# Expert pages of 64 rows, two to a block, ranked on the chip by expert

## The reference, cut to what matters

```python
probs = sigmoid(x @ router_w.T + expert_bias)          # (2048, 160)
top_w, top_idx = top_k(probs, 8)
top_w = top_w / (sum(top_w) + 1e-09) * 2.5
h1 = silu(einsum('th,eih->eti', x, w_gate))            # per expert 256 -> 128
routed = einsum('eti,ehi->th', h1 * combine.T, w_down) # per expert 128 -> 256
shared = silu(x @ w_gate_shared.T) @ w_down_shared.T
return x + routed + shared
```

## Time and profile before

| | |
|---|---|
| time, median of 3 runs | 1448.95 us (1445.54 to 1453.1) |
| span of the profiled execution | 1580.3 us |
| phase 1 and 2, in that execution | 1051 us |
| block loop with its fill and drain | 474 us |
| final sum and output | 55 us |
| HBM read and written | 161 MB and 100 MB |

### The profile page before, as it was taken

The page is one execution under the profiler, slowest core; times in us unless marked ns, Lnnn a source line. Parts: engine busy times, 40 slices in busy tenths (PEclk is TensorE's granted clock), DMA queues, the critical chain, the costliest instruction groups (busy, mean ns, idle before and its releaser), DMA issues. The chain is left out here.

```text
span 1580.3 us, 32555 instructions
## 1 busy us (share of the span) xinstructions
PE 1369.1 (87%) x10653; PEld 1008.8 (64%) x10653; DVE 996.6 (63%) x2910; ACT 618.7 (39%) x1909; POOL 615.5 (39%) x797
## 2 busy tenths in 40 slices
PE   7999999999987989999998998677787887878846
PEld 4666676666754666666666666466676776767645
DVE  3766666666653578867887787546665655544447
ACT  3544545444443566655665565221111111133100
POOL 1101111011101146555655555545556565555630
PEclk9999999999996899999999999889999999998978
DMA  8534244243400011111111111278878777776758
GB/s 257 191 98 142 92 142 138 95 141 100 134 1 28 14 53 53 51 63 63 50 54 64 63 36 40 70 235 266 248 232 245 233 236 250 239 218 204 227 195 351
DMA packets 153404, 221.57 MB, mean 140 GB/s; under 512 B 23789, under 2 KB 111116, under 8 KB 151320
## 3 DMA queue, kind: packets, MB, share of 16 engines
q1 hardware_dynamic: 53912, 97.83, 19.5%
q10 hardware_dynamic: 79456, 86.96, 17.6%
q0 software_dynamic: 19872, 34.71, 6.1%
HBM read 161.16 MB, written 99.61 MB: 165 GB/s over the span
## 5 line engine op out<-in xcount | busy, mean ns | idle before, releaser
L898 POOL DMA_INDIRECT y_d<-y,xg x286 | 278.6, 974 | 200.5 <-DVE y L895 126.7
L890 PE MATMUL bank<-pTC,ex 128*128 128x256 f32 x572 | 193.6, 423 | 73.2 <-ACT ex L884 41.0
L872 DVE COPY ex<-bank 128x256 f32<-128x256 f32 x286 | 120.4, 421 | 173.2 <-PE bank L868 101.9
L884 ACT ACTIVATE ex<-bank 128x128 f32<-128x128 f32 x286 | 77.6, 277 | 381.3 <-PE bank L880 222.0
L880 PEld LDWEIGHTS bank<-ex,pTC 128*128 128x128 f32 x1144 | 184.2, 207 | 51.2 <-issue 34.8
L880 PE MATMUL bank<-ex,pTC 128*128 128x128 f32 x1144 | 190.9, 293 | 17.4 <-issue 16.9
L890 PEld LDWEIGHTS bank<-pTC,ex 128*128 128x128 f32 x572 | 93.2, 205 | 91.0 <-ACT ex L884 48.9
L707 POOL DMA_INDIRECT xs_d<-xw,slot_id x128 | 131.0, 1023 | 34.6 <-issue 30.5
L895 DVE COPY y<-bank 128x256 f32<-128x256 f32 x286 | 120.5, 421 | 30.3 <-PE bank L890 18.1
L406 ACT ACTIVATE ex<-bank,nmC 128x256 f32<-128x256 f32 x256 | 119.5, 488 | 8.6 <-DVE nmC L400 8.1
L868 PE MATMUL bank<-ident,xg 128*128 128x128 f32 x572 | 116.0, 287 | 3.9 <-DMA xg<-xs_d 3.9
(11 more groups left out here) (308 smaller groups left out, 2919.5 us busy)
## 6 DMA issues: line engine op xcount, KB each, us to landing
pTC<-in_wexp SPq DMA_DIRECT2D x286, 256.0 KB
xs_d<-zeros ACTq DMA_DIRECT2D x16, 2448.0 KB, 9.7
xg<-xs_d ACTq DMA_DIRECT2D x143, 272.0 KB
cT<-in_ctx SPq DMA_DIRECT2D x32, 512.0 KB, 3.6
xg<-y_d SPq DMA_DIRECT2D x6, 1024.0 KB, 12.4
y_d<-y,xg POOLq DMA_INDIRECT x286
ex<-y_d SPq DMA_DIRECT2D x3, 1024.0 KB, 15.5
xf_d<-xw SPq DMA_DIRECT2D x16, 128.0 KB, 2.7
```

What stands on the lines that cost most here:

```text
L872: T.done("dve", dve.tensor_copy(xgT[z][:, :, :], bk[:, 0:2 * P].rearrange("p (c n) -> p c n", c=2)))
L884: U.done("act", act.activation(h[z][:, :], bk[:, 0:P], ACT.Silu))
L890: D.done("pe", pe.matmul(bk[:, 0:DIM], h[z][:, :], w[z][:, DIM:2 * DIM], start=True, stop=True))
L898: pool.indirect_dma_start(out=y_d, out_offset=bass.IndirectOffsetOnAxis(ap=who, axis=0), in_=y[:, n, :], in_offset=None, bounds_check=last ...
```

## The change

Pages have 64 rows (`PAGE`), and 416 of them cover the worst case; a block of the loop takes two pages, so there are 208 blocks instead of 286. A page may belong to any expert, so that a block has two.

- Rows carry no expert number any more. `stage_f` can give an expert one or two new pages in a tile (`gap`, `more`, `need`).
- `count_pages` computes per tile, on DVE, which expert owns each page, from the running sums.
- `order_pages` ranks the 416 pages by owner at the end of `phase2`: counts and comparisons on DVE, two groups of small matrix products on PE, and six operations on one partition, which write two tables into SBUF: for each place the expert and the page.
- The sorted list is cut into 16 slots of 26 pages. Block `d` of a turn of 8 blocks takes the next page of slots `2d` and `2d+1`; each slot has its own weight buffer of 256 KB. Where the next page has the same owner, 1000 is added to its number, so that the load is out of bounds and moves nothing. 16 buffers instead of 8 are made from `pT` and from weights of `phase2`.
- `load_weights` reads two numbers and issues two transfers on SP per block. `load_rows` does the same on ACT: two transfers of 64 rows, at page numbers out of the second table, 12 blocks ahead.
- `up` makes four products of 64 columns instead of two of 128, `down` two products with 64 stationary columns each, into the lower and the upper half of the PSUM rows.
- `common_up`, `common_down` and `common_out` have other due times, so that some of the shared expert's work falls beside the ordering.

```diff
+PAGE = 64
+SLOTS = 16
+TURNS = -(-((PAIRS + EXPERTS * (PAGE - 1)) // PAGE) // SLOTS)
+PAGES = SLOTS * TURNS
+BLOCKS = PAGES // 2
@@ stage_f
-            link(dve.tensor_tensor(need[:, :], after, room[:, :], ALU.is_gt))
+            dve.tensor_copy(ends[z][:, 0:1], ends[1 - z][:, EXPERTS:EXPERTS + 1])
+            link(dve.tensor_tensor(gap, after, room[:, :], ALU.subtract))
+            link(dve.tensor_scalar(more[:, :], gap, 0.0, None, ALU.is_gt))
+            link(dve.scalar_tensor_tensor(out=need[:, :], in0=gap, scalar=float(PAGE), in1=more[:, :], op0=ALU.is_gt, op1=ALU.add))
@@ count_pages
+            for n, c in enumerate(unsure):
+                last = dve.scalar_tensor_tensor(out=(late[:, :], spot[:, 0, :])[n % 2], in0=ends[j % 2][:, 1:], scalar=page[:, c:c + 1], ...
@@ order_pages
+            link(dve.tensor_reduce(keys[:, 0, :], counts[:, :, :], AX.X, ALU.add))
+            for c in range(CHUNKS):
+                last = pe.matmul(bank[7][:, c * P:(c + 1) * P], bc(keys[:, 0, c:c + 1], 1, P), ident[:, :], start=True, stop=True)
+            for c in range(CHUNKS):
+                last = dve.scalar_tensor_tensor(out=junk[c % 2], in0=row, scalar=keys[:, 1, c:c + 1], ...
+                        dve.tensor_scalar(onehot[k], numbers, ranks[:, k:k + 1], None, ALU.is_equal).then_inc(s_sort, 1)
+            for c in range(CHUNKS):
+                last = pe.matmul(bank[7][0:1, 0:PAGES], keys[:, 1, c:c + 1], onehot[c], start=(c == 0), stop=(c == CHUNKS - 1))
...
+            sp.wait_ge(s_table, 1)
+            for n in range(SLOTS // 2):
+                load_weights(nc, a, table, n, w, s_w)
@@ experts
+    _, which = nc.values_load_multi_w_load_instructions(table[0][0:1, 2 * n:2 * n + 2], engines=[mybir.EngineType.SP])
+    for half, e in enumerate(which):
+        sp.dma_start(w[2 * d + half], a["wexp"][bass.ds(e, 1)].rearrange("a p n -> (a p) n"), bounds_check="skip_entire_dma").then_inc(s_w[d], 16)
@@ load_rows
-            act.dma_start(xg[:, d % DOUBLES, :, :], doubles[steps[d]]).then_inc(s_g[d % DOUBLES], 16)
+            _, which = nc.values_load_multi_w_load_instructions(table[1][0:1, 2 * n:2 * n + 2], engines=[mybir.EngineType.Activation])
+            for half, q in enumerate(which):
+                act.dma_start(xg[half * PAGE:(half + 1) * PAGE, n % FETCHED, :], pages[bass.ds(q, 1)].rearrange("a p n -> (a p) n"), ...
@@ up
-            for c in range(2):
-                last = pe.matmul(bk[:, 0:P], w[z][:, c * P:(c + 1) * P], xgT[z][:, c, :], start=(c == 0), stop=(c == 1))
+            for half in range(2):
+                cols = slice(half * PAGE, (half + 1) * PAGE)
+                for c in range(2):
+                    last = pe.matmul(bk[:, cols], w[2 * z + half][:, c * P:(c + 1) * P], xgT[z][:, c, cols], start=(c == 0), stop=(c == 1))
@@ down
-            D.done("pe", pe.matmul(bk[:, 0:DIM], h[z][:, :], w[z][:, DIM:2 * DIM], start=True, stop=True))
+            for half in range(2):
+                rows = slice(half * PAGE, (half + 1) * PAGE)
+                last = pe.matmul(bk[rows, 0:DIM], h[z][:, rows], w[2 * z + half][:, DIM:2 * DIM], start=True, stop=True)
```

More of the change, by code:

```diff
@@ L122, in phase2_weights @@
     return (tern, wf, wqd, wod, wka, wkb, wva, wvb, bqd, bkd, bvd, bod, lns, lnb, wh, bh, bg, wqk, bqk, osw, osb, wout, bout,
-            wgs, wds, wr, be, tri, ones, base, pairs, half), loads
+            wgs, wds, wr, be, tri, ones, owner, page, pairs, half), loads
 class Turns:
@@ L225, in phase2 @@
         (tern, wf, wqd, wod, wka, wkb, wva, wvb, bqd, bkd, bvd, bod, lns, lnb, wh, bh, bg, wqk, bqk, osw, osb, wout, bout,
-         wgs, wds, wr, be, tri, ones, base, pairs, half) = resident
+         wgs, wds, wr, be, tri, ones, owner, page, pairs, half) = resident
         s_set, s_max = sem("s_set2"), sem("s_max")
@@ L264, in phase2 @@
         before = pair("before", [P, EXPERTS])
+        more = sb("more", [P, EXPERTS])
         need = sb("need", [P, EXPERTS])
         grown = sb("grown", [P, 2, EXPERTS])
-        ends = pair("ends", [P, EXPERTS])
-        room, lift, origin = sb("room", [P, EXPERTS]), sb("lift", [P, EXPERTS]), base
+        ends = pair("ends", [P, 1 + EXPERTS])
+        room, lift, origin = sb("room", [P, EXPERTS]), sb("lift", [P, EXPERTS]), sb("origin", [P, EXPERTS])
+        counts, expert, keys = sb("counts", [P, CHUNKS, TILES]), sb("expert", [P, CHUNKS]), sb("keys", [P, 2, CHUNKS])
         fresh = sb("fresh", [P, 2, EXPERTS])
@@ L271, in phase2 @@
         spot = sb("spot", [P, 2, EXPERTS])
-        whole = sb("whole", [P, TOPK], U32)
+        gap = spot[:, 1, :]
+        s_ids, s_pages, s_sort = sem("s_page_ids"), sem("s_pages"), sem("s_sort")
         s_common = [sem(f"s_common{z}") for z in range(3)]
@@ L710, in stage_f, with count_pages @@
                 grow(j)
-        def first_weights():
+        def count_pages(j):
+            yield 273.00
+            few, many = P * TOPK * j // PAGE, (P * TOPK * (j + 1) + EXPERTS * (PAGE - 1)) // PAGE
+            unsure = [c for c in range(CHUNKS) if P * (c + 1) > few and P * c < many]
+            for n, c in enumerate(unsure):
+                last = dve.scalar_tensor_tensor(out=(late[:, :], spot[:, 0, :])[n % 2], in0=ends[j % 2][:, 1:], scalar=page[:, c:c + 1],
+                                                in1=owner[:, :] if j < TILES - 1 else ones_e[:, :], op0=ALU.is_le, op1=ALU.mult, accum_out=counts[:, c, j:j + 1])
+                if n % 2 and c < unsure[-1]:
+                    link(last)
+            R.done(j, "dve", last, "counted")
+            R.wait(dve, "counted", j)
@@ L713, in first_weights @@
             yield 83.87
-            sp.wait_ge(s_rows[0], 16 * TOPK)
-            with nc.allow_non_contiguous_dma(reason="one word of each page"):
-                sp.dma_start(todo_row[0:1, 0:EARLY], page_words(xs_d)[0:1, 0:EARLY, :].rearrange("p q o -> p (q o)")).then_inc(s_todo, 16)
-            sp.wait_ge(s_todo, 16)
+            sp.wait_ge(s_table, 1)
+            E.wait(sp, "yo", TILES - 1)
             D.wait(sp, "pv", TILES - 1)
-            for r in range(EARLY):
-                load_weights(sp, a, todo_row, r, w[r], s_w[r])
+            for n in range(SLOTS // 2):
+                load_weights(nc, a, table, n, w, s_w)
@@ L929, in experts @@
             act.wait_ge(s_rows[z], 16 * TOPK * TILES // 2)
-        for d in range(AHEAD):
-            load_rows(d)
-        with nc.allow_non_contiguous_dma(reason="one word of each page"):
-            sp.dma_start(todo_row[0:1, EARLY:PAGES], page_words(xs_d)[0:1, EARLY:PAGES, :].rearrange("p q o -> p (q o)")).then_inc(s_todo, 16)
-        sp.wait_ge(s_todo, 32)
-        for b in range(PAGES + DOWN):
-            if EARLY <= b < PAGES:
+        for n in range(AHEAD):
+            load_rows(n)
+        for b in range(BLOCKS + DOWN):
+            if DEEP <= b < BLOCKS:
                 load(b)
-            if b % 2 == 0 and b // 2 + AHEAD < half:
-                load_rows(b // 2 + AHEAD)
+            if b + AHEAD < BLOCKS:
+                load_rows(b + AHEAD)
             if DOWN <= b:
                 down(b - DOWN)
-            if UP <= b < PAGES + UP:
+            if UP <= b < BLOCKS + UP:
                 up(b - UP)
-            if b < PAGES:
+            if b < BLOCKS:
                 turn(b)
@@ L953, in experts @@
         g = [v.rearrange("p (k n) -> p k n", k=TOPK) for v in g]
-        s_row = [sem(f"s_row{z}") for z in range(RING)]
+        s_row, used = s_w, TURNS * 32
         s_sum = [sem(f"s_sum{z}") for z in range(2)]
```

167 lines of the change are left out of this document (102 added, 65 removed).

## The result

| | before | after |
|---|---|---|
| time, median | 1448.91 us | 1834.89 us (1833.59 to 1835.9) |
| ratio after / before | | 1.2652, 95% interval 1.2625 to 1.2679 |

The changed kernel is 26.5% slower. I had forecast 1531 us (5.7% slower) in a range of 1450 to 1580, so the sign was right and the time lies 255 us above the range.

A forecast was written before the change was run, and what follows sets the result against it. The prediction took PE, at 1.10 us a block and the granted clock, to bound the loop before. Replacing its 343 us by 396 and adding 29 for routing, ordering and prologue gave 1449 - 343 + 396 + 29 = 1531 us, range 1450 to 1580.

The forecast's parts named there:

- The clock: Granted clock in the changed loop taken as 0.97, making 376 us at full clock into 388 us.
- `turn`, `up`, `down`: PE's work per block of the changed loop: 0.22 + 0.87 + 0.72 = 1.81 us at the full clock.
- rival 1: Weight loads in `up` are hidden, so `up` stays at 0.45 us and the total is 1445 us; chance 0.12.
- rival 3: Half-array products of `down` don't overlap: `down` 1.04 us, block 2.13 us, total 1600 us; chance 0.09.
- ACT: ACT's reads, row-transfer issues, waits and silu in the changed loop: about 1.45 us a block, below PE's 1.81.
- The loop before: Without the recording's stops, the old loop takes 343 us, bound by PE at 1.10 us a block and the granted clock.
- Routing: Added DVE operations per tile, some 2 us each, mostly hidden by PE's other work: 3 us in all, between 0 and 12.
- Ordering: Ranking pages after the last `spot`, then 16 first loads, delays the barrier to about 1058 us: 13 us, bounds 5 and 20.
- Prologue: 15 blocks' row transfers on ACT ahead of the loop's first silu take 18 us: loss 13 us, bounds 6 and 18.
- Transfers and the skip: Loop's weight loads fall from 207 to 120, 54 to 31 MB; transfers hidden under PE before and after, gain worth nothing.
- Rival 2: Transfers bound the loop before, which takes 435 us unrecorded; lighter traffic pays, total 1439 us or 1427; chance 0.13.
- rival 4: The skip does nothing: 329 pages load 256 KB each, the loop takes 423 us, total 1558 us; chance 0.02.

The follow-up runs named there:

- e14: Changed kernel with the rows of 5 blocks instead of 12 issued ahead of the loop: 1826.86 us.
- e15: Changed kernel without its skip, every page with pairs loading its weights: 1837.12 us.
- e4: Changed kernel with `up` as four products of 128 columns, silu taking its own 64, result unchanged: 1582.2 us in one recorded execution.
- e8: The kernel of e4 (changed kernel with full columns in `up`), timed without recording: 1556.72 us, ratio 1.0730 to the kernel before.
- e9: Changed kernel with full columns in `up`, rows of 5 blocks ahead, and second pages' row transfers on SP instead of ACT: 1580.33 us, ratio 1.0881.
- e16: Changed kernel with full columns in `up` and the rows of 5 blocks instead of 12 ahead of the loop: 1538.87 us, ratio 1.0590.
- e2: Changed kernel with `down` as one product on the whole array, second page's weights left out: 1578.2 us in one recorded execution.
- e7: Changed kernel with 32 more products of 512 columns on PE in the prologue, results unused: 1557.5 and 1804.3 us.
- e10: The kernel of e7 (32 more PE products in the changed kernel's prologue), four more executions: 1557.7, 1746.8, 1795.0 and 1602.4 us.
- e3: Changed kernel with `up` and `down` both as in the kernel before, second page's weights left out: 1575.9 us in one recorded execution.
- e12: The kernel before, unchanged, in one more recorded execution: span 1445.9 us, without stops.
- e6: The kernel before with every weight load behind the first eight out of bounds, moving nothing: 1448.48 us, ratio 0.9989.
- e11: The kernel before, scattering 32 rows instead of 128 in 78 of 286 blocks, whose pages hold no pair: 1443.78 us, ratio 0.9934.

## Why the prediction was wrong, step by step

- **The clock, the step that failed.** "With the stops gone and PE without gaps I take 0.97." It was 0.50. The mixture of both new forms, which comes at the low level out of the prologue, never regained the full one, in eight executions (the result, e14, e15). With full columns in `up` it did in all thirteen (e4, e8, e9, e16), with `down` on the whole array in the one of e2; e7 and e10 show that the level and not the work makes the time. What in the two forms together keeps it low, the runs don't show. Against the loop at the full clock (2.00 us a block, set by ACT) this is (3.365 - 2.004) x 207 = 282 us. My argument, PE without gaps, was read from products of the old forms; in the low loop PE was busy in 600 of 600 us. Nor did the prediction ask what PE's stop at the barrier would do to the clock. The Trainium skill (page "TensorE: Matmul & The Clock Gate", section "What's actually happening") puts it that recent busyness of PE releases the throttle. This case disagrees if busyness is what the profile counts: 100% at 0.50 in the changed kernel, 67% at 0.99 in e3.
- **`turn`, `up`, `down` in clock cycles: right.** 0.22 + 0.87 + 0.72 = 1.81 us forecast; 3.38 / 2 = 1.69 from the low level's block, 0.22 + 0.94 + 0.58 = 1.74 in e7. `up` is bound by its weight loads, so rival 1 falls. The Trainium skill (same page, section "LDWEIGHTS (loading the stationary operand)") makes a load's ns its columns divided by 1.2, an estimate of 107 ns for 128 columns. The 0.11 us a pair at the full clock agrees; at the low level a pair takes 0.22. `down` came out under my lower bound of 0.61, so rival 3 falls too, and the change of tile shape costs `down` less than I had read from the earlier trace rows; a part of it falls to `up`, whose first pair in e7 takes 0.16 us instead of 0.11.
- **ACT: too small.** 1.45 us a block forecast, 2.00 measured. I took SP's read of one number, 0.27, for ACT's read of two, which takes 0.50; the two issues take 1.28 with their register instructions where I had 1.06; and 0.18 lies between the silu and its neighbours in the queue. The silu's own work is mostly hidden, as I had it, but beside the read and not the issue. At the full clock ACT, and not PE, sets the block: (2.004 - 1.74) x 207 = 55 us over PE's own time. In the result it is hidden, because the clock was lower still.
- **The loop before: near in size, wrong in its bound.** 343 us forecast without stops, 374.5 measured from barrier to last scatter. The rows had it: 0.97 of scatter and 0.30 of issue is 1.27 us, which I used for after ("below 1.81") and did not hold against PE's 1.10 in before. Of the 134 us between the two spans of before, 35 lie ahead of the barrier (1051.5 and 1016.1), which I had put into the loop altogether; so 343 was 31 us short. Those 35 aren't stops that the trace calls "remote": from the first to the last `spot` the disturbed record takes 464.7 us and e12 434.0, without such a wait in either.
- **Routing: too small.** 3 us (0 to 12) forecast, 23.3 measured to the last `spot`. From the first to the last `spot` it is 18.7 us more (452.7 and 434.0), and DVE is busy for 18.9 more in that stretch (367.9 and 349.0). So the added operations cost 1.2 us a tile, less than my 2, but all of it shows; that the other tiles' work hides it was wrong. The other 4.6 us lie ahead of the first `spot`, as far apart as records of before and its variants are among themselves (565.6 to 570.3).
- **Ordering: right in the difference.** 13 us forecast, 14.3 measured. SP reads the table 17.9 us behind the last `spot` (I had 14.7), and its 16 loads end 11.7 us later, at 1052.5 (I had 11), with the barrier behind them. That the barrier fell at 1053.7, near my 1058, is luck: I had counted from a record whose last `spot` came 32 us too late, and the routing, which I had too small, and the ordering brought most of it back.
- **Prologue: too small.** 13 us (6 to 18) forecast, 20.8 measured; 30 transfers took 26.8 us of ACT where I had counted 18, by the same mis-sized read and issue:

```profile
1053.74 26.80 ACTq L919 DMA_DIRECT2D xg<-xs_d  x30
...
1080.59 0.28 ACT L945 ACTIVATE ex<-bank 128x128 f32<-128x128 f32 x1 [41.60 <-issue]
```

- **Transfers and the skip: right.** 120 loads for 31 MB (the 55 MB less than in e15 are 209 loads of the 329) and nothing gained: e15 shows it at the low clock and, for before, e6. Rival 2 (the transfers bound the loop before) falls with e6, rival 4 with the 75 MB of the weights' queue.
- **The sum with the measured terms:** 1445.9 + 23.3 + 14.3 + 20.8 + 3.365 x 207 - 366.1 - 0.3 = 1834.5 us. With the full clock's 414.8 in the loop it is 1552.7, near the 1557.5 of e7. That would have been inside my range, but in part by luck, with ACT's, the routing's and the prologue's terms too small and PE's too large. The sign doesn't hang on the clock: at the full one, in e8, the change is still 7.3% slower, only for ACT's sake and not, as I had it, for PE's.

## What to carry to other kernels

Cutting products in half doesn't only leave the number of weight loads as it was; it can leave PE fully occupied at half its clock. So when a change replaces full-width, full-array products by narrow and half-array ones, put the loop at 1.2 GHz among the rivals with a chance of its own, above all where PE stands before the loop (here the clock fell there), and look at whether one of the two forms can be kept wide at no cost, as `up` could here. Before pricing a saving, find which engine goes round without a pause in an undisturbed record: here it was the issue of one scatter a block on POOL, so fewer scatters were worth 50 us and nearly all of the weight traffic nothing. And where an engine issues transfers and also computes, count its register reads with the issues: here they were 1.78 of ACT's 1.96 us a block, and the silu had to wait behind them.

## What the runs showed of the hardware that I had not expected

- The same instruction stream runs at either level of the clock for hundreds of us: 1557.5 to 1804.3 us in six executions of one kernel, and 600 us at 0.50 with PE busy in all of them.
- Half-array products pair up better than I had read: four records of 256 columns on 64 stationary ones in 0.58 us at the full clock, where four one after the other on the whole array would be 0.86 (an estimate, twice the 0.43 for two in the earlier trace rows).
- A scatter of 32 rows keeps POOL nearly as long as one of 128, 0.88 us against 0.98 in e11, and the next starts 0.30 behind it.
- On ACT, reading two numbers into registers and issuing two transfers of 64 rows takes 0.50 + 1.28 = 1.78 us in e7. A silu of 0.28 us ahead of them falls mostly beside the read; the next one starts 0.10 behind the last issue.
